# Expert stage of a gated transformer block: gate and up products made transposed, with fewer copies on VectorE and 39 tiles in place of 40

## The chip, the core and the metric

The kernel runs on one core of a Trainium2 chip. The metric is the device time of one execution in microseconds (us); three runs of the kernel before gave 368.71, 369.37 and 370.10 us, median 369.37. Below, PE is TensorE, DVE is VectorE, ACT is ScalarE, POOL is GpSimd and SP is SyncE. An engine has a sequencer, which works through the engine's instruction stream in order (waits, register arithmetic, branches, and handing matmuls on), and the datapath behind it.

## What is computed

```
x = x + tanh(g_xattn[0]) * xattn_0(layernorm(x), ctx, Wq, Wkv)
x = x + tanh(g_ffn[0])   * ffn_0(layernorm(x), Wr, Wqkv, Wo)      # per expert: top 64 tokens, attention
x = x + tanh(g_xattn[1]) * xattn_1(layernorm(x), ctx, ctx, mask, Wq, Wk, Wv, Wo)
x = x + tanh(g_ffn[1])   * ffn_1(layernorm(x), ...)
# ffn_1, the stage that the change touches:
normed = (xt - mu) * rsqrt(var + 1e-5) * ln_gamma + ln_beta        # 2048 tokens of 128
probs  = softmax(normed @ router_w.T)                              # 8 experts
top_v, top_i = top_k(probs, 2);  gates = softmax(top_v)
for e in range(8):                                                 # gate_up_w[e]: (768, 128), down_w[e]: (128, 384)
    gate, up = split(normed @ gate_up_w[e].T)
    out += comb[:, e] * ((silu(gate) * up) @ down_w[e].T)
out += swiglu(normed, shared_gate_up_w, shared_down_w)
```

## The kernel before

Everything lives in one program; each engine has its own instruction stream, and the streams meet only through semaphores. After the second cross attention each token's normalised row is split into two float16 halves (a high part and a rest), and POOL sends it by indirect DMA (`send_rows`, L787) into a table in DRAM, `dispatched_rows`, one region for each expert. From the counts of each expert DVE works out which expert each tile of 128 rows belongs to (L1040 to L1072), packs the numbers of eight tiles into one word (`te_i`), and PE reads that word into a register. So the expert of a tile is known only at run time.

The expert stage then works through 40 tiles of 128 rows (4096 routed rows, with each expert's share rounded up to whole tiles). The weights are held in SBUF as a high and a low float16 part (`wh`, `wl`), and every product of two float32 operands is made of three float16 matmuls: high by high, high by low, low by high. The address of a weight slice is `w[:, ds(expert, 1), ...]` with the expert in a register, so PE's sequencer works out each address with register instructions that stand in the stream just before the matmul that needs it. For each group of three matmuls there are two such addresses (`wa` and `wb`). For one tile the work is, in order:

- SP (`load_slots`, L470 to L476) loads the 128 rows (`slot_rows`, four buffers), after the tile four before has been transposed and its destination made.
- PE (`step_pe`, L1453) transposes the two halves (2 matmuls, L1462); DVE copies them out to `slot_rows_t` (L1115).
- PE makes gate and up, tokens on the partitions: for each of the two, three matmuls of 384 columns (L1473 to L1475; in the profile all of them have the helper's line, L1160, and `slot_rows_t` as an operand). The rows are the stationary operand, the weights the moving one. This makes 2 groups of three and 4 addresses.
- ACT (`step_act`, L669) applies silu to gate (L681); DVE (`step_dve`, L1093) multiplies by up (L1128); ACT rounds the product to its high half (L676); DVE makes the rest (L1118).
- PE transposes the two halves of the product in 6 matmuls (L1482), since the hidden dimension has to be on the partitions for the next product; ACT copies them out (`region_x`, 128x768, L686).
- PE makes the down product in 9 matmuls of 128 columns (L1492 to L1494, helper line L1160, operand `region_x`): 3 groups of three and 6 addresses.
- DVE scales and copies the result (L1108) and makes the destination row numbers (L1100, L1123, L1110); POOL writes the rows back to DRAM by indirect DMA (L814, `expert_rows`). Rows that only pad a tile go to a dump area behind the 4096 real ones.

The order in each stream is written out by hand as a software pipeline. PE's step s holds, in this order, the row transposes of tile s+4, gate and up of tile s+3, the product's transposes of tile s+1 and the down product of tile s. Steps -4 to 7 are unrolled, with constants in the waits; steps 8 to 35 are a hardware loop of four steps in a round (L1513), where the thresholds of the waits are in registers too, with a load of the next packed word once in a round; the last steps are unrolled again. Behind the stage PE makes the second half of the shared expert (`shared_pe(SH, B)`, L1520), SP loads the written rows back (`region_q`), and DVE and POOL add them, weighted, to x (L1151), which is stored.

Of the kernel before, what the change touches and what calls it, by code (L numbers as in the profile page):

```python
# [9 lines left out]
I32 = mybir.dt.int32  # L10
# [23 lines left out]
TILES = 40  # L34
TTAB = TILES + 8
# [58 lines left out]
def build(nc, x_in, ctx_in, mask_in, gx_in, gf_in, wq0_in, wkv0_in, wr0_in, wv0_in, wo0_in, wk1_in,  # L94
# [3 lines left out]
    ytok = nc.dram_tensor("expert_rows", (2 * B * S + TILES * P + 1, D), F32).ap()  # L98
# [4 lines left out]
    with ExitStack() as ctx:  # L103
# [141 lines left out]
        tw = sb("tile_window", [P, TILES // 4, 8])  # L245
        tpack = sb("tile_pack", [P, TILES // 4])
        te_i = sb("tile_pack_i", [P, TILES // 4], I32)
# [7 lines left out]
        dbase = sb("slot_dest_base", [P, 1])  # L255
        dall = sb("slot_dest_of", [P, TILES])
        dst = sb("slot_dest", [P, 4], I32)
# [4 lines left out]
        hidt = xf[:, 0:2 * FF].bitcast(F16).rearrange("p (r n) -> p r n", r=2)  # L262
        xt_ps = bank[4][:, 0:P].bitcast(F16)
        ht_ps = bank[5][:, 0:FF].bitcast(F16)
# [138 lines left out]
        dest_base = sem("dest_base")  # L403
        rows_turned = sem("rows_turned")
        rows_turned_out = sem("rows_turned_out")
        gate_up_made = sem("gate_up_made")
# [3 lines left out]
        hidden_turned = sem("hidden_turned")  # L410
        hidden_turned_out = sem("hidden_turned_out")
# [17 lines left out]
        def _(eng):  # L429
# [50 lines left out]
            with eng.Fori(1, TILES // 4) as i:  # L480
                for r in range(4):
                    load_slots(4 * i + r, r)
            for r in range(4):
                eng.wait_ge(rows_sent[r], 16 * (TILES // 4))
# [12 lines left out]
        def _(act):  # L497
# [171 lines left out]
            def step_act(s, u):  # L669

                static = isinstance(s, int)
                if not static or 0 <= s + 2 < TILES:

                    act.wait_ge(hidden_done, s + 3)
                    wait(act, hidden_turned, s + 1)
                    act.activation(hsplit[:, u % 2, 0:FF], hid[:, u % 2, :], ACT.Copy).then_inc(hidden_high, 1)  # L676
                if not static or 0 <= s + 3 < TILES:
                    act.wait_ge(gate_up_made, s + 4)
                    wait(act, hidden_done, s + 2)
                    v = (u + 3) % 2  # L680
                    act.activation(sil[:, v, :], bank[2 * v][:, 0:FF], ACT.Silu, scale=1.0 / WS).then_inc(silu_done, 1)  # L681
# [6 lines left out]
            for s in range(-4, 8):  # L688
                step_act(s, s % 4)
            with act.Fori(2, TILES // 4 - 1) as i:  # L690
                for u in range(4):
                    step_act(4 * i + u, u)
            for s in range(TILES - 4, TILES + 1):
# [15 lines left out]
        def _(pool):  # L709
# [97 lines left out]
            due = pool.alloc_register("tiles_due")  # L807
            pool.reg_mov(due, 1)
            with pool.Fori(0, TILES // 4):
                for r in range(4):  # L810

                    pool.wait_ge(rows_ready, due)
                    pool.reg_add(due, due, 1)
                    pool.indirect_dma_start(ytok, bass.IndirectOffsetOnAxis(dst[:, r:r + 1].bitcast(U32), 0),  # L814
                                            yv[:, r, :], None).then_inc(rows_sent[r], 16)
# [10 lines left out]
        def _(dve):  # L826
# [127 lines left out]
            for stage, t in skewed(NT, C_EVERY, C_DVE):  # L954
# [51 lines left out]
                elif stage == "route" and t % T == T - 1:  # L1006
# [9 lines left out]
                    dve.tensor_copy(pay[:, n, D + 1], ef[:, :, 0])  # L1016
# [44 lines left out]
            for h in range(2):  # L1061
                last = dve.tensor_scalar(tw[:, :, 4 * h:4 * h + 4],
                                         te[:, 4 * h:4 * h + TILES].rearrange("p (i j) -> p i j", j=4),
# [3 lines left out]
                                   c32[:, C_P8:C_P8 + 8].rearrange("p (a j) -> p a j", a=1).to_broadcast((P, TILES // 4, 8)),  # L1067
# [533 lines left out]
```

## Time and profile before

| what | us |
|---|---|
| median of three runs | 369.37 |
| span of the profiled execution | 368.7 |
| PE busy (matmuls) | 274.0 |
| DVE busy | 251.1 |
| ACT busy | 213.6 |
| POOL busy | 151.1 |
| first gate and up matmul of the expert stage | starts at 252.75 |
| last gate and up matmuls (tile 39) | start at 340.29 |
| last indirect DMA of the stage | starts at 348.02 |

```text
span 368.7 us, 7937 instructions
## 1 busy us (share of the span) xinstructions
PE 274.0 (74%) x2143; PEld 202.4 (55%) x2144; DVE 251.1 (68%) x884; ACT 213.6 (58%) x503; POOL 151.1 (41%) x201
## 2 busy tenths in 40 slices
PE   3499880395899876899897862536999999999810
PEld 2398780153677554577575751223776676776510
DVE  3256259996577631778889966833988788887475
ACT  1555549775577595845763534301877777777430
POOL 2412358960222510811732677760344444444502
PEclk9999996589899968999898855655999999999975
DMA  7860000620000000000000011221222122221173
GB/s 187 272 260 0 3 0 9 221 93 0 3 1 2 1 2 0 3 0 2 0 3 7 32 52 44 88 75 44 53 59 63 54 58 58 58 58 36 46 239 103
DMA packets 19469, 21.06 MB, mean 57 GB/s; under 512 B 3184, under 2 KB 17008, under 8 KB 18800
## 3 DMA queue, kind: packets, MB, share of 16 engines
q1 hardware_dynamic: 16992, 15.79, 14.1%
q0 software_dynamic: 2304, 4.77, 4.0%
q8 instruction: 14, 0.23, 0.3%
q10 hardware_dynamic: 144, 0.15, 0.2%
q14 instruction: 15, 0.12, 0.1%
HBM read 14.28 MB, written 6.42 MB: 56 GB/s over the span
## 4 chain that ended last, share of the span: by engine, by line
PE 54%; DVE 18%; issue 7%; POOL 7%; DMA 5%; ACT 5%; SPq 2%; DVEq 0%; POOLq 0%; ACTq 0%
PE bank L1160 43%; POOL dispatched_rows L787 5%; PE bank L1482 3%; DVE x L1151 2%; DMA region_q<-expert_rows 2%; DMA wr<-in 2%; DVE region_k L883 2%; PE bank L1462 2%; DVE region_k L967 2%; DVE top L882 2%; DVE nm L965 1%; ACT x_hat L514 1%; PE bank L1213 1%; PE bank L1196 1%; DVE bn_raw L838 1%
## 5 line engine op out<-in xcount | busy, mean ns | idle before, releaser
L814 POOL DMA_INDIRECT expert_rows<-region_k,slot_dest x40 | 38.2, 955 | 63.3 <-DVE slot_dest L1110 62.4
L1160 PE MATMUL bank<-w_high,slot_rows_t 128*128 x160 | 47.2, 337 | 3.2 <-issue 1.9
L681 ACT ACTIVATE region_w<-bank 128x384 f32<-128x384 f32 x40 | 19.6, 490 | 35.6 <-PE bank L1160 34.8
L787 POOL DMA_INDIRECT dispatched_rows<-region_t,slot x32 | 31.9, 997 | 16.1 <-issue 9.2
L1160 PE MATMUL bank<-w_high,region_x 128*128 (+1 forms) x272 | 35.8, 228 | 2.3 <-DVE region_t L908 2.1
L1128 DVE SCALAR_TENSOR_TENSOR region_w<-bank,region_w 128x384 f32<-128x384 f32 x40 | 22.3, 557 | 16.4 <-ACT region_w L681 15.3
L686 ACT ACTIVATE region_x<-bank 128x768 f16<-128x768 f16 x40 | 32.2, 804 | 0.9 <-PE bank L1482 0.9
L729 POOL TENSOR_SCALAR minus_mean_rstd<-mean_var 128x4 f32<-128x4 f32 x16 | 3.4, 213 | 71.1 <-DVE mean_var L841 45.7
L740 POOL TENSOR_TENSOR w_low<-w_scaled,w_high 128x512 f16<-128x512 f32 (+1 forms) x23 | 29.0, 1286 | 0.0
L514 ACT ACTIVATE x_hat<-x,minus_mean_rstd,rstd 128x128 f32<-128x128 f32 x64 | 26.2, 482 | 4.4 <-POOL minus_mean_rstd L732 4.4
L1160 PE MATMUL bank<-w_low,region_x 128*128 (+1 forms) x136 | 27.1, 227 | 0.0
L1160 PE MATMUL bank<-w_low,slot_rows_t 128*128 x80 | 26.9, 336 | 0.0
L1160 PEld LDWEIGHTS bank<-w_high,region_x 128*128 128x128 f16 x272 | 23.7, 98 | 3.2 <-issue 2.6
L1160 PEld LDWEIGHTS bank<-w_high,slot_rows_t 128*128 128x128 f16 x160 | 16.0, 100 | 14.4 <-issue 8.6
L1118 DVE TENSOR_TENSOR region_k<-region_w,region_k 128x384 f16<-128x384 f32 x40 | 22.3, 557 | 1.5 <-ACT region_k L676 1.4
L772 POOL TENSOR_TENSOR region_w<-region_k,rope_b 128x128 f32<-128x128 f32 x16 | 7.4, 463 | 36.4 <-DVE rope_b L926 36.4
L676 ACT ACTIVATE region_k<-region_w 128x384 f16<-128x384 f32 x40 | 20.9, 523 | 1.6 <-DVE region_w L1128 1.2
L1482 PE MATMUL bank<-c,region_k 128*128 128x128 f16 x240 | 19.9, 219 | 0.7 <-ACT region_x L686 0.7
L1482 PEld LDWEIGHTS bank<-c,region_k 128*128 128x128 f16 x240 | 16.6, 98 | 5.9 <-issue 1.0
L1160 PEld LDWEIGHTS bank<-v_blocks,region_k 128*128 128x128 f32 x128 | 17.9, 216 | 3.1 <-ACT region_k L631 1.7
L1160 PE MATMUL bank<-v_blocks,region_k 128*128 128x36 f32 x128 | 18.5, 295 | 0.8 <-DVE region_x L976 0.7
L634 ACT ACTIVATE region_k<-region_k 128x512 f32<-128x512 f32 x16 | 10.0, 628 | 15.6 <-DVE region_k L967 15.6
(238 smaller groups left out, 785.0 us busy)
## 6 DMA issues: line engine op xcount, KB each, us to landing
w_scaled<-in SPq DMA_DIRECT2D x5, 1024.0 KB, 8.2
slot_rows<-dispatched_rows SPq DMA_DIRECT2D x40, 65.5 KB, 1.9
region_q<-expert_rows SPq DMA_DIRECT2D x4, 512.0 KB, 5.7
x<-in SPq DMA_DIRECT2D x4, 256.0 KB, 4.4
region_w<-in SPq DMA_DIRECT2D x2, 512.0 KB, 6.9
out<-x SPq DMA_DIRECT2D x4, 256.0 KB, 2.6
w_scaled<-in SPq DMA_DIRECT2D x1, 704.0 KB, 4.0
expert_rows<-region_k,slot_dest POOLq DMA_INDIRECT x40, 2.2
```

The source lines that it names most:

```text
L514: last = act.activation(xh[:, t, :], x[:, t, :], ACT.Identity, bias=nmr[:, t:t + 1], scale=rstd[:, t:t + 1])
L634: act.activation(e1[:, t % 2, :], e1[:, t % 2, :], ACT.Exp, scale=HD ** -0.5).then_inc(cross1_exp, 1)
L676: act.activation(hsplit[:, u % 2, 0:FF], hid[:, u % 2, :], ACT.Copy).then_inc(hidden_high, 1)
L681: act.activation(sil[:, v, :], bank[2 * v][:, 0:FF], ACT.Silu, scale=1.0 / WS).then_inc(silu_done, 1)
L686: act.activation(hidt[:, (u + 1) % 2, :], ht_ps, ACT.Copy).then_inc(hidden_turned_out, 1)
L740: pool.tensor_tensor(wl[:, c], wf[:, r], wh[:, c], ALU.subtract).then_inc(w_low_done, 1)
L787: pool.indirect_dma_start(disp, bass.IndirectOffsetOnAxis(slot[:, b * T + t, c:c + 1].bitcast(U32), 0), pay[:, b * T + t, :], None).then_i ...
L814: pool.indirect_dma_start(ytok, bass.IndirectOffsetOnAxis(dst[:, r:r + 1].bitcast(U32), 0), yv[:, r, :], None).then_inc(rows_sent[r], 16)
L1118: dve.tensor_tensor(hsplit[:, u % 2, FF:2 * FF], hid[:, u % 2, :], hsplit[:, u % 2, 0:FF], ALU.subtract).then_inc(hidden_low, 1)
L1128: dve.scalar_tensor_tensor(hid[:, v, :], bank[2 * v + 1][:, 0:FF], 1.0 / WS, sil[:, v, :], ALU.mult, ALU.mult).then_inc(hidden_done, 1)
L1160: return pe.matmul(o, l, r, start=start, stop=stop)
L1482: last = pe.transpose(ht_ps[:, i * P:(i + 1) * P], hsplit[:, (u + 1) % 2, i * P:(i + 1) * P], ident16)
```

## The change

Of the expert stage and its tables only:

- Gate and up are made transposed: the weights are now the stationary operand and the rows the moving one. The 768 columns of gate and up are cut into 6 pieces of 128, and each piece is a group of three matmuls of 128 columns, with a `wa` and a `wb` of its own. The result has the hidden dimension on the partitions.
- The six transposes of the product, the copy behind them (L686) and its two semaphores are gone; the down product reads `hsplit` itself.
- The copy of the transposed rows moves from DVE to ACT, and the bank that holds them is doubled (banks 4 and 5), for which PE waits once, ahead of the stage, for the shared expert's first sums (`sh_added`).
- The pipeline is one step shorter: row transposes of tile s+3, gate and up of s+2, down of s. Silu waits for gate alone (`gate_made`), the product for up (`up_made`).
- The destination is one instruction on POOL (`slot_dest`) for each tile, two tiles ahead, and the three instructions on DVE are gone. POOL's loop is unrolled. Padding rows get a row number above the last real one, and the indirect DMA skips them (`bounds_check`).
- 39 tiles in place of 40 (the largest number that 4096 rows in 8 experts can need); the last round has three steps.

```
-TILES = 40
-TTAB = TILES + 8
+TILES = (2 * B * S + E * (P - 1)) // P
+ROUNDS = -(-TILES // 4)
+TTAB = 4 * ROUNDS + 8
...
             def step_act(s, u):
+                if not static or 0 <= s + 3 < TILES:
+                    act.wait_ge(rows_turned, s + 4)
+                    wait(act, up_made, s + 2)
+                    act.activation(xdt[:, (u + 1) % 2, :], xt_ps[(u + 1) % 2], ACT.Copy).then_inc(rows_turned_out, 1)
+                if not static or 0 <= s + 1 < TILES:
+                    act.wait_ge(hidden_done, s + 2)
+                    wait(act, down_made, s)
+                    act.activation(hsplit[:, (u + 1) % 2, 0:FF], hid[:, (u + 1) % 2, :], ACT.Copy).then_inc(hidden_high, 1)
                 if not static or 0 <= s + 2 < TILES:
...
-                    act.wait_ge(hidden_turned, s + 2)
-                    wait(act, down_made, s)
-                    act.activation(hidt[:, (u + 1) % 2, :], ht_ps, ACT.Copy).then_inc(hidden_turned_out, 1)
...
+            def slot_dest(n):
+                pool.wait_ge(rows_loaded[n % 4], n // 4 * 16 + 16)
+                pool.tensor_scalar(dst[:, n:n + 1], xd[:, n % 4, D + 1:D + 2], te[:, n:n + 1], xd[:, n % 4, D:D + 1],
+                                   ALU.is_equal, ALU.add).then_inc(dest_ready, 1)
+            slot_dest(0)
+            slot_dest(1)
+            for n in range(TILES):
+                if n + 2 < TILES:
+                    slot_dest(n + 2)
+                pool.wait_ge(rows_ready, n + 1)
+                pool.wait_ge(dest_ready, n + 1)
+                pool.indirect_dma_start(ytok, bass.IndirectOffsetOnAxis(dst[:, n:n + 1].bitcast(U32), 0),
+                                        yv[:, n % 4, :], None, bounds_check=2 * B * S - 1, oob_is_err=False).then_inc(rows_sent[n % 4], 16)
...
-            def step_pe(s, u, expert, expert3):
+            def step_pe(s, u, expert, expert2):
...
-                    for i in range(2):
-                        o = bank[2 * v + i][:, 0:FF]
-                        wa, wb = (w[:, ds(expert3, 1), i * FF:(i + 1) * FF].rearrange("p e n -> p (e n)") for w in gu_w)
-                        mm(o, xa, wa, True, False)
-                        mm(o, xa, wb, False, False)
-                        last = mm(o, xb, wa, False, True)
-                    last.then_inc(gate_up_made, 1)
-                if not static or 0 <= s + 1 < TILES:
-                    pe.wait_ge(hidden_low, s + 2)
-                    wait(pe, hidden_turned_out, s + 1)
-                    for i in range(2 * FC):
-                        last = pe.transpose(ht_ps[:, i * P:(i + 1) * P], hsplit[:, (u + 1) % 2, i * P:(i + 1) * P], ident16)
-                    last.then_inc(hidden_turned, 1)
+                    for i in range(NF):
+                        o = bank[2 * v + i // FC][:, i % FC * P:(i % FC + 1) * P]
+                        wa, wb = (w[:, ds(expert2, 1), i * P:(i + 1) * P].rearrange("p e n -> p (e n)") for w in gu_w)
+                        mm(o, wa, xa, True, False)
+                        mm(o, wa, xb, False, False)
+                        last = mm(o, wb, xa, False, True)
+                        if i == FC - 1:
+                            last.then_inc(gate_made, 1)
+                    last.then_inc(up_made, 1)
                 if not static or 0 <= s < TILES:
-                    pe.wait_ge(hidden_turned_out, s + 1)
+                    pe.wait_ge(hidden_low, s + 1)
                     wait(pe, rows_ready, s - 1)
...
-                        hi = hidt[:, u % 2, i * P:(i + 1) * P]
-                        lo = hidt[:, u % 2, FF + i * P:FF + (i + 1) * P]
+                        hi = hsplit[:, u % 2, i * P:(i + 1) * P]
+                        lo = hsplit[:, u % 2, FF + i * P:FF + (i + 1) * P]
...
+            pe.wait_ge(sh_added, SH)
```

## Rows read from the trace of the kernel before

**Rows 1.** Waits, 263 to 335 us, PE and ACT: total us, times, longest.

```profile
PE bank L1160 <- issue: 1.5, 9, 0.2
...
ACT region_w L681 <- PE bank L1160: 18.5, 31, 1.1
```

**Rows 2.** Chain that ended last, in order of time: start, length, what.

```profile
261.04 1.15 PE bank L1160 x6
...
269.20 1.04 PE bank L1160 x6
...
303.90 1.15 PE bank L1160 x6
...
313.05 1.15 PE bank L1160 x6
```

**Rows 3.** Timeline of PE in one loop step: start, length, line, operation, tiles, idle before.

```profile
315.05 0.33 PE L1160 MATMUL bank<-w_high,slot_rows_t 128*128 x1
315.22 0.33 PE L1160 MATMUL bank<-w_low,slot_rows_t 128*128 x1
...
317.26 0.23 PE L1462 MATMUL bank<-c,slot_rows 128*128 128x128 f16 x1 [0.23 <-issue]
```

**Rows 4.** Source line L1160, 303.9 to 322.2 us: register instructions of two rounds.

```profile
L1160 PEldq ALU_OP  x66: 32/36/36, 303.9 to 322.0; - x66
...
L1160 PEldq FUSED_REGOPS  x40: 46/46/60, 304.0 to 322.1; - x40
```

**Rows 5.** Source line L424, the wait helper, same stretch.

```profile
L424 PEldq EVENT_SEMAPHORE  x18: 51/51/51, 306.4 to 321.6; - x18
L424 PEldq ALU_OP  x14: 32/32/36, 304.3 to 321.8; - x14
```

**Rows 6.** Timeline: a down product (register addresses), then the shared expert (fixed addresses).

```profile
344.85 0.22 PE L1160 MATMUL bank<-w_low,region_x 128*128 x1
...
345.33 0.22 PE L1160 MATMUL bank<-w_low,region_x 128*128 x1
...
350.99 0.22 PE L1160 MATMUL bank<-w_low,region_k 128*128 128x128 f16 x1
...
351.16 0.22 PE L1160 MATMUL bank<-w_low,region_k 128*128 128x128 f16 x1
```

**Rows 7.** Groups of ACT and DVE, 303.9 to 322.2 us: busy, mean ns | idle before.

```profile
L676 ACT ACTIVATE region_k<-region_w 128x384 f16<-128x384 f32 x9 | 4.7, 523 | 0.0
L681 ACT ACTIVATE region_w<-bank 128x384 f32<-128x384 f32 x8 | 3.9, 491 | 5.0 <-PE bank L1160 5.0
...
L1128 DVE SCALAR_TENSOR_TENSOR region_w<-bank,region_w 128x384 f32<-128x384 f32 x8 | 4.5, 558 | 3.4 <-ACT region_w L681 3.2
L1118 DVE TENSOR_TENSOR region_k<-region_w,region_k 128x384 f16<-128x384 f32 x8 | 4.4, 556 | 0.0
L1108 DVE TENSOR_SCALAR region_k<-bank 128x128 f32<-128x128 f32 x8 | 2.3, 287 | 0.0
```

**Rows 8.** Timeline of POOL: small instructions between two indirect DMAs.

```profile
219.77 0.19 POOL L729 TENSOR_SCALAR minus_mean_rstd<-mean_var 128x4 f32<-128x4 f32 x1 [0.23 <-DVE mean_var L987]
...
221.78 1.10 POOL L787 DMA_INDIRECT dispatched_rows<-region_t,slot  x1 [0.16 <-issue]
```

**Rows 9.** Timeline: end of the stage.

```profile
340.29 0.34 PE L1160 MATMUL bank<-w_high,slot_rows_t 128*128 x1
...
348.02 0.96 POOL L814 DMA_INDIRECT expert_rows<-region_k,slot_dest  x1 [0.30 <-issue]
```

**Rows 10.** Timeline: start of the stage, gate and up of tile 0.

```profile
252.75 0.50 PE L1160 MATMUL bank<-w_high,slot_rows_t 128*128 x1
...
253.37 0.85 PE L1160 MATMUL bank<-w_high,slot_rows_t 128*128 x2
```

**Rows 11.** Stretches: busy and count of PE, PEld, DVE, ACT, POOL; granted clock.

```profile
89.25:92.66 3.41, 1.34 (x21) 1.16 (x20) 2.49 (x4) 0.00 (x0) 0.00 (x0) 1.00 0.00 0
92.66:96.08 3.42, 3.10 (x20) 2.44 (x19) 1.11 (x6) 1.30 (x7) 0.90 (x2) 0.50 0.00 0
```

More of the change, by code:

```diff
@@ L261, in build @@
         hsplit = region_k[:, 0:2, 0:FF].bitcast(F16)
-        hidt = xf[:, 0:2 * FF].bitcast(F16).rearrange("p (r n) -> p r n", r=2)
-        xt_ps = bank[4][:, 0:P].bitcast(F16)
-        ht_ps = bank[5][:, 0:FF].bitcast(F16)
+        xt_ps = [bank[4 + r][:, 0:P].bitcast(F16) for r in range(2)]
         yv = region_k[:, 2, :].rearrange("p (r n) -> p r n", r=4)
@@ L482, in _ @@
                     load_slots(4 * i + r, r)
+            for n in range(TILES // 4 * 4, TILES):
+                load_slots(n, n % 4)
             for r in range(4):
-                eng.wait_ge(rows_sent[r], 16 * (TILES // 4))
+                eng.wait_ge(rows_sent[r], 16 * len(range(r, TILES, 4)))
             for b in (0, B - 1, *range(1, B - 1)):
@@ L671, in step_act @@
                 static = isinstance(s, int)
-                if not static or 0 <= s + 2 < TILES:
[L674 to L681, printed above, removed]
-                if not static or 0 <= s + 1 < TILES:
-                    act.wait_ge(hidden_turned, s + 2)
-                    wait(act, down_made, s)
-                    act.activation(hidt[:, (u + 1) % 2, :], ht_ps, ACT.Copy).then_inc(hidden_turned_out, 1)
-            for s in range(-4, 8):
+                if not static or 0 <= s + 3 < TILES:
[6 more added lines that the diff above has]
+                    act.activation(hsplit[:, (u + 1) % 2, 0:FF], hid[:, (u + 1) % 2, :], ACT.Copy).then_inc(hidden_high, 1)
+                if not static or 0 <= s + 2 < TILES:
+                    act.wait_ge(gate_made, s + 3)
+                    wait(act, hidden_done, s + 1)
+                    act.activation(sil[:, u % 2, :], bank[2 * (u % 2)][:, 0:FF], ACT.Silu, scale=1.0 / WS).then_inc(silu_done, 1)
+            for s in range(-3, 8):
                 step_act(s, s % 4)
-            with act.Fori(2, TILES // 4 - 1) as i:
+            with act.Fori(2, ROUNDS - 1) as i:
                 for u in range(4):
                     step_act(4 * i + u, u)
-            for s in range(TILES - 4, TILES + 1):
+            for s in range(4 * (ROUNDS - 1), TILES):
                 step_act(s, s % 4)
@@ L1460, in step_pe @@
                     for h in range(2):
[L1461 to L1462 removed]
+                        w = xd[:, r, h * (D // 2):(h + 1) * (D // 2)].bitcast(F16)
+                        last = pe.transpose(xt_ps[r % 2][:, h * P:(h + 1) * P], w, ident16)
                     last.then_inc(rows_turned, 1)
[L1464 to L1468 removed]
+                if not static or 0 <= s + 2 < TILES:
+                    pe.wait_ge(rows_turned_out, s + 3)
+                    wait(pe, hidden_done, s + 1)
+                    v = u % 2
@@ L1500, in _ @@
             load_window(1)
-            for s in range(-4, 4):
-                step_pe(s, s % 4, e[max(s, 0)], e[max(s + 3, 0)])
+            pe.wait_ge(sh_added, SH)
+            for s in range(-3, 4):
+                step_pe(s, s % 4, e[max(s, 0)], e[max(s + 2, 0)])
             def round_pe(i, ahead):
                 e = experts()
-                for u in range(4 if ahead else 5):
-                    step_pe(4 * i + u, u % 4, e[u], e[u + 3])
+                for u in range(4 if ahead else TILES - 4 * i):
+                    step_pe(4 * i + u, u, e[u], e[u + 2])
                     if ahead and u == 1:
```

92 lines of the change are left out of this document (30 added, 62 removed).

## Prediction

> **What bounds the kernel now.** The page first: in the slices of the expert stage (252 to 348 us) PE stands at 9 of 10, DVE at 7 to 8, and PE's clock is fully granted. So PE is the engine to look at, and the question is what in PE. The waits of the stage come next [rows 1]: ACT waits for PE (18.5 us), while PE waits for another engine hardly at all; what idle time it has is called "issue". The chain of the end then gives the pace. From one loop round to the next, tile by tile at the same place, 303.90 to 313.05, are 9.15 us for four tiles, 2.29 each; in the unrolled rounds 261.04 to 269.20 are 8.16 us, 2.04 each [rows 2]. The array doesn't need that much. Matmuls of 384 columns start 0.17 us apart [rows 3] and those of 128 columns with fixed addresses 0.17 us for three, 0.056 each [rows 6]. A tile has 6 of the first kind and 17 of the second (2 row transposes, 6 transposes of the product, 9 of down): 6 x 0.17 + 17 x 0.056 = 1.97 us. Some 0.32 us in each loop tile is neither array nor wait for an engine; a part of it is seen as a gap ahead of the next tile's first matmul, 0.23 us at 317.26, released by nothing [rows 3].
>
> What fills it is PE's sequencer. Line L1160 holds, in two rounds, 66 + 40 register instructions, and the wait helper another 32 instructions [rows 4, 5]. The price of those is seen where PE has nothing queued. At the end of the stage the down product of one tile, three groups of three matmuls with two addresses each, has its w_low matmuls at 344.85 and 345.33, two groups apart, so 0.24 us for a group; the same three matmuls with fixed addresses, in the shared expert, take 0.17 (350.99 to 351.16) [rows 6]. A group with register addresses can't be issued faster than 0.24 us. Now the sum for a round: 20 groups (5 a tile) x 0.24 = 4.8 us, 32 transposes at no more than 0.056 = 1.8 us, and 106 + 32 - 80 = 58 further register and wait instructions in two rounds, 29 in one, besides the load of the next word and the branch, for the 2.55 us that remain: under 0.09 us each, against 0.24 - 0.17 = 0.07 visible for the two in a group. The round is full. I read the stage as bound by PE's sequencer, with the array fed from a queue that the long 384-column matmuls fill and the short ones empty.
>
> **The change, part by part, per tile.**
> - Gate and up: 2 groups become 6, so 4 groups more, + 4 x 0.24 = +0.96 us of sequencer. For the array 6 x 0.17 = 1.02 become 18 x 0.056 = 1.01: nothing.
> - The six product transposes go: at most 6 x 0.056 = 0.34; at least nothing, as a matmul without an address may cost the sequencer little. I take 0.17.
> - Of eight waits in PE's step two go (for the copy behind those transposes and ahead of down). Each is worth 0 (it rides on an instruction that stays) to 0.09; I take 0.1 for both.
> - Net +0.69 a tile, with ends of +0.96 (nothing given back) and +0.96 - 0.34 - 0.18 = +0.44. Loop tiles go from 2.29 to 2.98 (2.73 to 3.25), unrolled ones from 2.04 to 2.73.
> - The load of the packed word and the branch stay once in a round.
> - ACT loses the 0.8 us copy and gets the copy of 256 columns, no more than its 0.49 for 384 [rows 7]: at most 0.49 + 0.52 + 0.49 = 1.5 us a tile. DVE keeps 0.56 + 0.56 + 0.29 = 1.41 [rows 7]. Both lie under the pace; they cost nothing as long as it is above 1.5.
> - POOL: 0.96 for the DMA, then 0.23 to a small instruction, 0.19 for it, and 0.16 to the next DMA [rows 8, 9], 1.54 a tile with the destination. What is queued behind a wait there is only the next tile's send. The bounds check isn't in the trace; a tile may cost 0 to 0.5 more and is hidden up to 2.9, by PE. SP's loads wait for that destination of four tiles before, some three steps (9 us) ahead of use: hidden; at a pace of 1.6 it would be near.
> - Skipped padding rows (some 900 of 4992) take writes away that nobody waits for: nothing. The wait for `sh_added` stands ahead of rows that land at 251.5, and POOL's first two destinations stand behind its last dispatch: nothing.
> - A shorter pipeline: down of a tile comes two steps (6 us) after its gate; silu, product and split take 0.49 + 0.56 + 0.52 + 0.56 = 2.1 [rows 7]. Hidden.
>
> The stage. Tile 0's gate and up start at 252.75 as now [rows 10]. The first two steps hold gate and up alone and run at the half clock: 384 columns take 0.31 there (252.75 to 253.37 for two [rows 10]), so 128 take 0.105, and 18 + 2 of them 2.1; two steps 4.2. Then 36 steps reach tile 38's gate and up: 8 unrolled x 2.73 = 21.8, 28 in the loop and behind it x 2.98 = 83.4. That is 362.2 us, where the last one starts at 340.29 now [rows 9]: +21.9 us. From there to the last indirect DMA are 7.73 us now [rows 9]. After: 6 groups 1.44, then 0.2 for the result, 0.56 + 0.52 + 0.56 (silu is done by then) with three handovers of 0.05, down 0.72 + 0.2, copy 0.29, and 0.5 until POOL's DMA starts: 5.2 us. That gives 2.5 back; POOL's queue at the end (0.30 idle, a DMA behind a DMA, [rows 9]) is gone too. The last DMA starts at 367.4 in place of 348.02, +19.4 us; what follows (landing, load, sum, store) is the same. Profiled execution: 368.7 + 19.4 = 388.1; the median of the runs is 0.7 above the span, so 389 us.
>
> The Trainium skill has two rules here, and they don't agree. "TensorE: Matmul & The Clock Gate", section "Wait — 56ns, not 53.3ns?", has a warm matmul cost its columns at 2.4 GHz and 2.5 ns; by it 29 matmuls of 128 columns are an estimated 1.62 us a tile, and the stage is far faster than now (the first rival). The section "Back-to-back issue gap" of that page of the Trainium skill gives about 81 ns for each 128-column matmul with its weight load; by it a tile takes an estimated 29 x 0.081 = 2.35 us, much as now (the third rival). The fixed-address rows agree with the first (0.056) and not with the second; neither section knows of address arithmetic.
>
> **The rivals.**
> - *The array sets the pace* (the side of faster). If the address arithmetic of gate and up overlaps with matmuls that are queued, a tile costs 29 x 0.056 = 1.62 us, above POOL's 1.54. Tile 38 starts at 252.75 + 4.2 + 36 x 1.62 = 315.3, the last DMA at 320.5: 27.5 us earlier, 342 us. For it: in steady state today's down products do run at the array's pace, since 384-column matmuls fill the queue ahead of them. Against it: after the change there are no long matmuls left to fill it, and the loop round is already longer than the array needs. It decides from the pace at which both kernels are equal: (348.02 - 5.2 - 252.75 - 4.2) / 36 = 2.39 us a tile. Below that the change is a gain.
> - *The clock falls.* The array has work for 1.62 of 2.98 us. At 89.25 to 92.66 us PE was busy for 1.34 of 3.41 us at the full clock, and the next stretch ran at half, 1.2 in place of 2.4 GHz [rows 11]. At half clock a tile is 29 x 0.105 = 3.05 us of array, and with what the queue can't hide 3.1 to 3.3: 36 x 0.25 = 9 us at the most behind the forecast, 394 to 398 us. Against it: PE had been idle for over half of the stretch before that drop, in long waits, and has only short gaps here; and the half clock, if it comes, leaves the array no gaps.
> - *Only the groups count.* If waits and the other register instructions lie beside matmuls, a tile is 9 x 0.24 + 2 x 0.056 = 2.27 us, 2.44 with the word's load and the branch (about 0.7 a round). At 2.27 the last DMA starts at 343.9 (365 us), at 2.44 at 350.0 (371 us); 368 us in the middle, no change. Against it: the same reckoning gives 1.65 a tile now, where 2.29 are measured.
> - *The change doesn't do what it says*, in that two addresses for each piece are made with fewer register instructions than in down: it would fall in with the third or the first case.
>
> **How the numbers follow.** Forecast (sequencer, 2.98 a tile): 0.66. Clock falls: 0.12. Groups only: 0.06. Array: 0.16, the fourth case among it. The forecast's own range follows from 2.73 to 3.25 in the loop: -9 and +10 us, 380 to 399 with the clock's case inside it. I take 379 to 399, which leaves out the two fast cases and little else. What a measurement can tell from no change is 0.5%, 1.8 us. Slower by more: 0.66 + 0.12 + 0.02 = 0.80; within: 0.04; faster: 0.16.
>
> **What the profile would show.** Right: PE's busy share in the stage falls, the w_low matmuls of the gate and up groups (`slot_rows_t`) stand about 0.24 us apart, loop rounds of some 12 us, PE's idle time still called "issue", DVE, ACT and POOL idle a good half. L1160 has 9 fused register instructions a tile. Wrong: three matmuls of gate and up in 0.17 us throughout and a round under 9.5 us; or ACT or POOL with no idle time; or a granted clock of 0.5 in the stage, which makes the second rival out of the forecast. The prediction hangs on one number, the 0.24 us for a group with two register addresses, read at the end of the stage, and on its holding for addresses of the stationary operand too, which the trace of before doesn't show.

## The result, and the profile after

Slower: a median of 397.99 us (396.41 to 399.08, four runs) where the kernel before, beside it on the same chip, took 369.74 (368.71 to 371.25, four runs). The ratio is 1.073, 95% interval 1.067 to 1.080. The profiled execution of after is 394.6 us long, that of before 368.7. The forecast was a profiled execution of 388.1 and a median of 389 us.

The first look is the page of after, its slices (tenths busy in 40 slices of 9.9 us; the stage is slices 26 to 38).

```profile
span 394.6 us, 8358 instructions
...
PE   3599760786998468998798362498888888888830
...
DVE  4156179975677317887998674154444445444566
ACT  2555559682776868466554421253333434333330
POOL 3313179911225108034347877135545454545412
PEclk9999995698999979998895556599999999999975
```

PE stays the busiest engine, at 8 of 10 now; DVE fell from 7 or 8 to 4 or 5 and ACT to 3 or 4. TensorE's clock was fully granted from slice 27 to the end of the stage (1.00, the level of 2.4 GHz, from 263 to 362 us), so the half clock of the rival has no part in the loss.

The chain that ended last gives the pace. Columns: start, length, what. One place of the loop's round comes back as the first three rows:

```profile
299.66 1.58 PE bank L1147 x18
...
312.32 1.57 PE bank L1147 x18
...
324.97 1.57 PE bank L1147 x18
...
368.74 1.54 PE bank L1147 x18
...
375.02 2.11 DMA expert_rows<-region_k,slot_dest
```

A round of four tiles is 12.65 us, 3.16 a tile, where [rows 2] have 9.15 and 2.29. Tile 0's gate and up start at 252.65, where [rows 10] have 252.75; the last gate and up start at 368.74 and the last indirect DMA at 375.02, where [rows 9] have 340.29 and 348.02: 28.4 and 27.0 us later.

What PE waits for is in the waits of the stage, 270 to 360 us (total, times, longest):

```profile
ACT slot_rows_t L673 <- PE bank L1450: 46.9, 29, 2.1
POOL expert_rows L816 <- DVE region_k L1112: 42.7, 28, 2.1
DVE region_k L1115 <- ACT region_k L678: 25.3, 28, 1.3
...
PE bank L1147 <- issue: 8.3, 37, 0.3
```

ACT, POOL and, through ACT, DVE wait for PE; PE has gaps only for "issue": in 90 us now 8.3 at these matmuls and 4.6 at the row transposes (L1450), where in 72 us before has 1.5 [rows 1] and 1.6 (L1462). The rest of the loss is no gap in this view: it lies between the groups. The timeline of PE, one tile's gate and up:

```profile
359.54 0.22 PE L1147 MATMUL bank<-slot_rows_t,w_low 128*128 128x128 f16 x1
...
359.78 0.22 PE L1147 MATMUL bank<-slot_rows_t,w_low 128*128 128x128 f16 x1
...
360.01 0.22 PE L1147 MATMUL bank<-slot_rows_t,w_low 128*128 128x128 f16 x1
...
360.74 0.22 PE L1147 MATMUL bank<-slot_rows_t,w_low 128*128 128x128 f16 x1
```

Each of the six groups of three matmuls has one w_low matmul; they stand 0.24 us apart, as in the down product of before, and not 0.17 as with fixed addresses [rows 6]. A busy row of 0.22 us hides this: the matmuls overlap in the array, and only the distance between starts tells. The source line of the matmuls, two rounds (299.66 to 324.95 us), shows what stands between them:

```profile
L1147 PEldq ALU_OP  x94: 32/32/36, 299.7 to 324.7; - x94
L1147 PEldq FUSED_REGOPS  x72: 46/46/60, 299.8 to 324.9; - x72
```

Nine fused instructions a tile, one for each group, where [rows 4] have five. The same view of a part of one tile's gate and up (359.55 to 360.75 us) shows when they start:

```profile
L1147 PEldq FUSED_REGOPS  x5: 46/46/46, 359.6 to 360.5; - x5
L1147 PEldq ALU_OP  x5: 32/32/32, 359.7 to 360.6; - x5
```

Five of each kind in turn, from 359.6 to 360.6 us: a fused one every 0.24 us and an ALU_OP halfway between. So a register instruction starts about every 0.12 us all through the groups, though its own row is only 32 or 46 ns long. What fills the rest of the 0.12 us isn't shown.

### The profile page after: what moved, and what is told of

It reads as the page before. It is cut to its first block, busy times and chain, and to the rows that moved or that the text cites. A ratio compares the mean times of both kernels' runs of the same rounds, so it can differ in the third digit from the quotient of the medians.

```text
span 394.6 us, 8358 instructions
## 1 busy us (share of the span) xinstructions
PE 287.0 (73%) x2354; PEld 211.1 (53%) x2355; DVE 233.2 (59%) x721; ACT 197.5 (50%) x500; POOL 173.5 (44%) x239
## 4 chain that ended last, share of the span: by engine, by line
PE 56%; DVE 16%; issue 10%; ACT 6%; POOL 6%; DMA 5%; SPq 2%; DVEq 0%; POOLq 0%; ACTq 0%
PE bank L1147 48%; POOL dispatched_rows L783 5%; PE bank L1450 2%; DMA wr<-in 2%; DVE x L1138 2%; DMA region_q<-expert_rows 2%; DVE region_k L885 2%; DVE region_k L969 1%; DVE top L884 1%; DVE nm L967 1%; ACT x_hat L511 1%; ACT w_high L523 1%; PE bank L1200 1%; PE bank L1183 1%; ACT w_scaled L521 1%
## 5 line engine op out<-in xcount | busy, mean ns | idle before, releaser
L1147 PE MATMUL bank<-slot_rows_t,w_high 128*128 128x128 f16 x468 | 59.2, 227 | 8.5 <-issue 8.5
L1147 PE MATMUL bank<-slot_rows_t,w_low 128*128 128x128 f16 x234 | 52.0, 223 | 0.0
L673 ACT ACTIVATE slot_rows_t<-bank 128x256 f16<-128x256 f16 x39 | 14.9, 383 | 67.2 <-PE bank L1450 67.2
L1147 PE MATMUL bank<-w_high,region_k 128*128 (+1 forms) x266 | 39.2, 230 | 11.3 <-DVE region_k L1085 7.3
L1115 DVE TENSOR_TENSOR region_k<-region_w,region_k 128x384 f16<-128x384 f32 x39 | 24.0, 615 | 32.2 <-ACT region_k L678 32.2
L1147 PEld LDWEIGHTS bank<-slot_rows_t,w_high 128*128 x468 | 28.3, 100 | 24.9 <-issue 14.7
L1147 PEld LDWEIGHTS bank<-w_high,region_k 128*128 128x128 f16 x266 | 26.0, 100 | 20.5 <-issue 9.7
L1147 PE MATMUL bank<-w_low,region_k 128*128 (+1 forms) x133 | 29.8, 225 | 0.0
L1147 PEld LDWEIGHTS bank<-slot_rows_t,w_low 128*128 x234 | 23.0, 98 | 0.4
L1450 PE MATMUL bank<-c,slot_rows 128*128 128x128 f16 x78 | 11.1, 224 | 12.9 <-DMA slot_rows<-dispatched_rows 7.9
L1112 DVE TENSOR_SCALAR region_k<-bank 128x128 f32<-128x128 f32 x39 | 11.3, 291 | 13.1 <-PE bank L1147 13.0
```

The costliest lines, as they stand in the source:

```text
L673: act.activation(xdt[:, (u + 1) % 2, :], xt_ps[(u + 1) % 2], ACT.Copy).then_inc(rows_turned_out, 1)
L1112: dve.tensor_scalar(yv[:, r, :], bank[6 + r % 2][:, 0:D], 1.0 / WS, None, ALU.mult).then_inc(rows_ready, 1)
L1115: dve.tensor_tensor(hsplit[:, v, FF:2 * FF], hid[:, v, :], hsplit[:, v, 0:FF], ALU.subtract).then_inc(hidden_low, 1)
L1147: return pe.matmul(o, l, r, start=start, stop=stop)
L1450: last = pe.transpose(xt_ps[r % 2][:, h * P:(h + 1) * P], w, ident16)
```

## The experiments

The theory that stands to be tested: PE's sequencer sets the pace of the stage in both kernels, and the two register instructions of each group are what it spends its time on. The rivals: the array sets it; the group count has nothing to do with it, and another part of the change lost the time; the waits and the loop are what costs. "Pace" below is the distance between the same rows of two rounds in the chain, divided by four.

**1 to 3: the addresses taken away.** In three kernels the weights are read at a fixed address, always those of the first expert, so nearly all of PE's register instructions in the groups fall away and nothing else changes. In the first, of after, for all groups:

```
-wa, wb = (w[:, ds(expert2, 1), i * P:(i + 1) * P]...   gate and up
+wa, wb = (w[:, 0:1, i * P:(i + 1) * P]...
-wa, wb = (w[:, ds(expert, 1), i * D:(i + 1) * D]...    down
+wa, wb = (w[:, 0:1, i * D:(i + 1) * D]...
```

> The changed kernel, but every weight slice of the expert stage is read at the fixed address of expert 0, so no address of a matmul stands in a register; the same matmuls, waits, copies and DMAs. What it leaves out: the right expert's weights (the routed sum is made with expert 0's). Theory (PE's sequencer with its register instructions sets the pace): a group of three matmuls goes from 0.24 to 0.17 us, the loop tile from 3.16 us to the next bound, which by this kernel's trace is POOL with 1.18 + 0.38 + 0.23 + 0.16 = 1.95 us: some 36 x 1.15 = 41 us less, about 357 us. Rival A (it is the number of 128-column matmuls and weight loads, at 0.08 us each): at least 29 x 0.08 = 2.3 us a tile, 367 us or more. Rival B (ACT, DVE or a load sets the pace): no change, 398 us.

In the second, of after, for gate and up alone:

> The changed kernel with fixed addresses (expert 0) for the gate and up weights alone; the down product keeps its register addresses. What it leaves out: the right expert's gate and up weights. Theory: 12 of the 18 register instructions for addresses go, 6 groups x (0.24 - 0.06) = 1.05 us of sequencer a tile: 3.16 to 2.1 us, 36 x 1.05 = 38 us less, about 360 us. Rival A (matmul count): as in the kernel with all addresses fixed. Rival B: no change.

In the third, of before, for all groups (its `expert3` and FF columns in place of `expert2` and P):

> The kernel before with the fixed addresses of expert 0 for all weights. What it leaves out: the right expert's weights. Theory: the sequencer loses 10 address instructions a tile, and the array becomes the bound at 6 x 0.163 + 17 x 0.056 = 1.93 us, with DVE's 1.9 close to it: 2.24 to about 2.0 us, 39 x 0.24 = 9 us less, about 360 us. Rival (the stage before was bound by the array or by DVE's chain and not by the sequencer): no change, within 1 us of 369.5.

Measured, in two executions each, beside 371.89 us for the kernel before: 355.93 us (ratio 0.957, 0.944 to 0.970), 358.02 (0.962, 0.946 to 0.979) and 358.48 (0.964, 0.950 to 0.978). In all three the rivals, with 367 or 398 us for the first two and no change for the third, are outside. So the whole loss of the change, and more, hangs on the addresses: by the ratios (1.073 and 0.957 of 371 us) after is some 43 us faster without them than with them, before 13. With gate and up alone freed, 41 of the 43 are back. The chain of before with fixed weights shows an even pace that the array sets:

```profile
294.16 0.98 PE bank L1160 x6
296.08 0.97 PE bank L1160 x6
298.01 0.97 PE bank L1160 x6
```

1.92 us a tile; the prediction had worked out 1.97 for what the array needs. From 263 to 325 us PE is busy throughout and waits for nothing; DVE, busy for 59.8 of the 62 us, is close behind. After with fixed weights ran at the array's pace in a few tiles only:

```profile
265.60 1.51 PE bank L1147 x27
267.33 1.51 PE bank L1147 x27
268.97 1.51 PE bank L1147 x27
```

267.33 to 268.97 is 1.64 us for the 29 matmuls of a tile, 0.057 each; the first rival had 1.62. The w_low matmuls of gate and up, whose weights are the stationary operand, stand 0.17 us apart here, where the changed kernel has 0.24:

```profile
265.55 0.22 PE L1147 MATMUL bank<-slot_rows_t,w_low 128*128 128x128 f16 x1
265.72 0.22 PE L1147 MATMUL bank<-slot_rows_t,w_low 128*128 128x128 f16 x1
```

The section "Back-to-back issue gap" of the page "TensorE: Matmul & The Clock Gate" of the Trainium skill, about 81 ns for such a matmul with its weight load, would make that an estimated 2.35 us; this row doesn't agree, and the 0.24 us for three in the changed kernel, which looks like it, is gone as soon as the addresses are. But this pace didn't last. POOL in the same kernel, 263 to 330 us (count | busy, mean ns | idle before):

```profile
L816 POOL DMA_INDIRECT expert_rows<-region_k,slot_dest x35 | 39.6, 1133 | 11.4 <-POOL slot_dest L806 7.4 <-DVE region_k L1112 3.2 <-issue 0.8
L806 POOL TENSOR_SCALAR slot_dest<-slot_rows,tile_expert 128x1 int32<-128x1 f32 x34 | 15.4, 452 | 1.7
```

35 tiles in 67 us, 1.91 each, and of the 67 POOL waits 3.2 for the result of another engine. Its DMA, its destination and the handover between the two fill the rest, and the row loads, which wait for the destinations, now come late for PE (waits, 270 to 330 us):

```profile
PE bank L1450 <- DMA slot_rows<-dispatched_rows: 5.1, 8, 1.3
```

So the part of the change that moved the destinations to POOL costs nothing in the changed kernel, where PE hides it, and would be the next bound at 1.9 us a tile if PE were faster.

**4: register additions in before**, four in each step, ahead of gate and up:

```
+for _ in range(4):
+    pe.reg_add(idle, idle, 1)
```

> The kernel before with four more register additions on PE in each tile's step (a register that nothing reads), ahead of gate and up; the same matmuls and the same output. Theory: each costs the sequencer about 0.1 us and all of it is on the path: 40 x 0.4 = +16 us, about 385 us. Rival (the sequencer has slack): 0 to +2 us, 370 us.

Measured: 371.88 us beside 371.89, ratio 1.000 (0.996 to 1.005). It isn't a test. The source line of the groups has 66 ALU_OP and 40 FUSED_REGOPS rows in two rounds (296.33 to 314.76 us), as without the edit [rows 4]: the compiled program doesn't hold the additions, whose result nobody reads. It says only that two builds of the same work agree.

**5: waits in before**, for a count reached long ago:

```
+for _ in range(4):
+    pe.wait_ge(tiles, 3)
```

> The kernel before, with four waits added on TensorE at the start of every step of the expert loop; what they wait for is long reached, so nothing is held up but the sequencer. If TensorE's sequencer sets the pace and a wait costs it about 0.1 us, the loop's tiles go from 2.29 to about 2.6 us and the time rises by 10 to 16 us, to some 383 us where the kernel before takes 370. If the instructions between the groups lie beside the array's work (the array needs 1.9 us a tile), nothing changes: 370 us.

Measured: 377.99 us beside 372.06, ratio 1.017 (1.012 to 1.021); pace 9.94 us a round (299.84 to 309.78) in place of 9.15. The direction is the theory's, and an instruction that holds nothing up but the sequencer costs time; but it is 0.79 us for the 16 waits added to a round, 0.05 each and not 0.1. The compiled loop doesn't hold 16 more instructions. In two rounds (299.84 to 309.78 is one):

```profile
L1469 PEldq EVENT_SEMAPHORE  x20: 51/51/51, 301.5 to 319.3; - x20
L424 PEldq EVENT_SEMAPHORE  x14: 51/51/51, 302.4 to 318.9; - x14
```

These are 34 where [rows 5] have 18, with the 14 ALU_OP of that line unchanged: 8 more in a round, 0.10 us for each. The chain of this run goes through ACT's silu and DVE's product in some tiles, where it puts PE's gap down to L1128. That isn't a wait: the matmuls of 307.15 stand behind the product of two tiles before, which began at 303.74 and took 0.56 us.

**6 and 7: the loop written out.** PE's rounds 2 to 8, in before and in after; the upper bound is `TILES // 4 - 1` in before and `ROUNDS - 1` in after:

```
-with pe.Fori(2, ...) as i:
+for i in range(2, ...):
```

> The kernel before, with TensorE's loop over rounds 2 to 8 written out step by step: the same groups, waits and expert numbers in registers, but no jump and no threshold that has to be computed into a register. Theory of the sequencer: the 28 tiles go from 2.29 us each to the 2.04 us of the steps that were written out already, 7 us less, 362 to 363 us. Rival (the array, or a chain through the other engines, sets the pace): no change.

> The changed kernel with the same edit. Its loop tiles take 3.16 us, its written-out ones 2.85 to 3.05. Theory of the sequencer: 28 tiles x 0.2 = about 6 us less, 391 to 392 us, and still far above the kernel before, because the addresses in the groups stay. If the loop were the whole of the loss, it would come back to 370 us.

Measured: before 367.44 us beside 372.06 (0.988, 0.984 to 0.993), after 393.81 (1.057, 1.049 to 1.066). Before gains 4.6 us (1.2%) where 7 were expected; its pace is 8.92 a round (292.52 to 328.21 are four rounds), so 2.23 a tile and not 2.04. Written out, a round has 71 instructions of the sequencer's in place of 74, counted over all lines, so there was little to gain. After went from 1.073 to 1.057 of before, in two different comparisons, some 6 us, with 12.1 us a round in place of 12.65. So the loop itself is a small part of the pace in both kernels, and no part of the difference between them.

**8: fewer steps in before**: rounds written out, two covered waits of each step dropped, the expert's number kept in a register for the down product three steps later.

```
+if 0 <= s + 3 < TILES:
+    held[s + 3] = expert3 = pe.snap(expert3, min_val=0, max_val=E - 1)
+if 0 <= s < TILES:
+    expert = held.pop(s)
...
-pe.wait_ge(rows_turned_out, s + 4)
+if s + 4 >= TILES:
+    pe.wait_ge(rows_turned_out, s + 4)
...
-pe.wait_ge(hidden_turned_out, s + 1)
+if s + 1 >= TILES:
+    pe.wait_ge(hidden_turned_out, s + 1)
```

> The kernel before with the rounds written out, two waits of each step left out that another wait of the same step already covers, and each tile's expert number put into a register once and kept for the down projection three steps later. Theory of the sequencer: below the 2.04 us a tile of the written-out steps, by about 0.1 us, with a floor at the 1.92 us of the kernel with fixed weights: 358 to 361 us, and faster than both kernels. Rival: the kept registers or code that grows long cost as much as they save, and it stays at the 362 us of the written-out kernel or above.

Measured: 361.71 us, ratio 0.975 (0.970 to 0.980), faster than both kernels, with nothing left out. The chain:

```profile
303.30 1.15 PE bank L1160 x6
...
311.47 1.15 PE bank L1160 x6
```

8.17 us for four tiles, 2.04 each, with 56 + 40 + 16 instructions of the sequencer's in two rounds where the written-out kernel of run 6 has 66 + 40 + 32. That is 13 fewer in a round for 0.75 us; it is 0.12 us a tile above the array's 1.92, so part of what was saved was no longer on the path.

**9: the small groups alone.** This run takes from the change only the number of groups. The rows stay stationary, the transposes, copies and waits stay; the 384 columns are made in three groups of 128.

```
-for i in range(2):
-    o = bank[2 * v + i][:, 0:FF]
-    wa, wb = (w[:, ds(expert3, 1), i * FF:(i + 1) * FF]...
+for i in range(NF):
+    o = bank[2 * v + i // FC][:, i % FC * P:(i % FC + 1) * P]
+    wa, wb = (w[:, ds(expert3, 1), i * P:(i + 1) * P]...
```

> The kernel before, with nothing changed but the cut of gate and up: the rows stay the stationary operand, but the 384 columns of each product are made in three groups of 128, so six groups a tile in place of two, with twelve register addresses in place of four. Columns for the array, transposes, copies and waits are as before. Theory of the sequencer: 4 more groups x 0.24 = 0.96 us a tile, loop tiles of 3.25 us, and 38 of them 36 us more: about 408 us, slower than the changed kernel. Rival (the array sets the pace, or the loss lies in the other parts of the change): 370 to 375 us.

Measured: 405.44 us beside 370.6, ratio 1.091 (1.084 to 1.099). The chain and, under it, the source line of two rounds:

```profile
300.04 1.65 PE bank L1160 x18
...
364.77 1.68 PE bank L1160 x18
```

```profile
L1160 PEldq ALU_OP  x98: 32/32/36, 300.1 to 325.8; - x98
...
L1160 PEldq FUSED_REGOPS  x72: 46/46/60, 300.2 to 325.9; - x72
```

300.04 to 364.77 are five rounds of 12.95 us: 3.24 a tile, 0.95 more than before. The columns that the array has to stream are the same. Four groups cost 0.95 us, 0.24 each, and they bring exactly 16 ALU_OP and 16 fused instructions in a round more than [rows 4], so 0.119 us for one register instruction. They also bring 12 more matmuls and weight loads a tile, which this run can't tell from the addresses; runs 1 and 2, where as many matmuls without addresses run at 0.057 us each, and run 10 can. With them it is settled: one part of the change makes the whole loss and more, and it makes it in a kernel that has nothing else of the change.

**10: one address instead of two.** In after, gate and up read the low half of the weights at a fixed address, that of the first expert; what this leaves out is the right expert's low half.

```
-wa, wb = (w[:, ds(expert2, 1), i * P:(i + 1) * P]... for w in gu_w)
+wa = gu_w[0][:, ds(expert2, 1), i * P:(i + 1) * P]...
+wb = gu_w[1][:, 0:1, i * P:(i + 1) * P]...
```

> The changed kernel, in which gate and up read the low half of the weights at a fixed address (so always those of the first expert) and the high half at the expert's: one register address a group in place of two, the same matmuls. With both fixed the kernel took 358 us, with both in registers 398. If each register instruction costs its own time, about 0.09 us, the six fewer of a tile give 0.5 us back: loop tiles of about 2.6 us, 378 to 381 us. If a group pays once for having any register address (a queue that is emptied), it stays at about 398 us.

Measured: 372.48 us beside 370.6, ratio 1.005 (1.001 to 1.009). The chain has one round at

```profile
301.45 1.74 PE bank L1147 x27
...
311.34 1.74 PE bank L1147 x27
```

9.89 us, 2.47 a tile in place of 3.16. The six register instructions that a tile has less are worth 0.69 us, 0.115 each; I had expected 0.5 (0.09 each). That the cost goes by instruction and not by group is shown, with the number of matmuls unchanged, and its size agrees with that of run 9. In its source line the fused ones are 72 as in after and the ALU_OP 46 in place of 94: the second address of a group is the ALU_OP, the first the fused one.

**11: 39 tiles**, on top of run 8, the part of the change that could help: the tables, the loads, the sends and the last rounds for 39 tiles, groups and destinations as in before.

```
-TILES = 40
+TILES = (2 * B * S + E * (P - 1)) // P
```

> The kernel before with fewer register steps (361.7 us beside 372 for the kernel before), and from the change only that 39 tiles are worked on in place of 40; TensorE's groups, the transposes and the destinations stay as they were. One step of 2.05 us falls away at the end of the stage: about 359.5 us, ratio 0.969 to the kernel before. Rival: the last tile's rows weren't what the end waited for, and it stays at 361.7 us, 0.975.

Measured: 358.08 us, ratio 0.966 (0.960 to 0.971), the fastest kernel that reads every expert's own weights. One step of 2.05 us is 0.6% of it; against run 8 (0.970 to 0.980, in another comparison) it is some 1% less, with intervals that just touch, so the gain of this step is likely and not proven.

**12: the six transposes given back to after**, without copy and wait:

```
+for i in range(2 * FC):
+    pe.transpose(bank[6 + u % 2][:, P:P + FF].bitcast(F16)[:, i * P:(i + 1) * P],
+                 hsplit[:, u % 2, i * P:(i + 1) * P], ident16)
```

> The changed kernel, to which the six transposes of the product are given back, into a part of the bank that nobody reads; they bring no wait, no copy and no register address. It prices by itself what the forecast took as 0.17 us a tile between ends of 0 and 0.34. If they cost the array's full time, 39 tiles take 13 us more, about 411 us; at the forecast's half of it 6.6 us, about 404; if the matmuls lie wholly beside the sequencer's work, nothing: 398 us. The kernel before with small groups (3.24 us a tile with transposes and waits, 3.16 after) speaks for under 0.1 us, so for 398 to 401 us.

Measured: 399.52 us beside 371.48, ratio 1.076 (1.072 to 1.080), where after had 1.073 (1.067 to 1.080). In the chain

```profile
299.81 1.56 PE bank L1147 x18
...
338.70 1.55 PE bank L1147 x18
```

three rounds take 38.89 us, 3.24 a tile in place of 3.16. Six transposes, 0.34 us of the array, are worth 0.08 us a tile here: most of them run while the sequencer works on addresses.

## Why the prediction was right, and where it was off

**The bound.** Right. A pace that the sequencer sets was read from a remainder of 0.32 us a tile that neither array nor engines explained, and from one number at the end of the stage. Runs 3, 5 and 8 move the pace of before by the sequencer's work alone (1.92, 2.49 and 2.04 in place of 2.29), runs 1, 9 and 10 that of after and of its groups.

**Four groups x 0.24.** Right: forecast 0.96 us a tile, measured alone 0.95 (run 9). That the price would hold for addresses of the stationary operand, which the trace of before couldn't show, is seen in the 0.24 between the w_low rows of after.

**What is given back.** This is the term that was mis-sized. The forecast took off 0.17 for the six transposes and 0.1 for two waits, 0.27 in all, and had 2.98 in the loop. After is at 3.16; the small groups in before are at 3.24. So everything else of the change gives back 0.08 us a tile, and run 12 finds just that for the transposes. The low end that I had named for the waits, nothing, is what happened. The wait helper (now L419) has 18 EVENT_SEMAPHORE rows in two rounds in after as in [rows 5] and 6 ALU_OP in place of 14, but the other 8 stand, for PE's other waits, on lines of their own, so it is 32 in both:

```profile
L1454 PEldq ALU_OP  x6: 32/32/32, 302.0 to 324.4; - x6
L1446 PEldq FUSED_REGOPS  x2: 46/46/46, 308.2 to 320.8; - x2
```

The step that was off is "at most the array's 0.34, at least nothing, I take half": in a stage that I had just called bound by the sequencer, the array's price of a matmul was the wrong end to lean on. The error is 28 x 0.18 = 5.0 us in the loop and 1.5 in the rest of the stage, together the 6.5 us by which the last gate and up came late (368.74 against 362.2).

Counted over all lines of PE's sequencer, the branch and the load of the next word among them, after has 208 instructions in two rounds and before 148: 30 more in a round, for 3.5 us more, 0.117 each, which accounts for the whole loss in the loop.

A small thing doesn't fit and stays open. Run 9 has 212, so after has 2 fewer in a round. At 0.119 these are 0.24 us, and run 12, which has the same transposes as run 9 and the same 208 instructions as after, should have a round shorter by that; its rounds are 12.96 us and those of run 9 are 12.95. Nor is the price the same for every kind: the waits of run 5 cost 0.10, and what run 8 took away gave 0.06 each.

**The tail.** From the last gate and up to the last indirect DMA the forecast had 5.2 us, it was 6.3. Two steps were off: "POOL's queue at the end is gone", and a product that goes straight on to ACT. The timeline of after's end:

```profile
370.37 0.56 DVE L1104 SCALAR_TENSOR_TENSOR region_w<-bank,region_w 128x384 f32<-128x384 f32 x1 [0.94 <-PE bank L1147]
...
371.38 0.52 ACT L678 ACTIVATE region_k<-region_w 128x384 f16<-128x384 f32 x1 [1.30 <-PE bank L1147]
...
372.39 1.06 POOL L816 DMA_INDIRECT expert_rows<-region_k,slot_dest  x1 [1.57 <-DVE region_k L1112]
372.42 0.28 DVE L1112 TENSOR_SCALAR region_k<-bank 128x128 f32<-128x128 f32 x1
...
373.56 0.29 DVE L1112 TENSOR_SCALAR region_k<-bank 128x128 f32<-128x128 f32 x1 [0.86 <-PE bank L1147]
...
373.75 0.97 POOL L816 DMA_INDIRECT expert_rows<-region_k,slot_dest  x1 [0.30 <-issue]
...
375.02 0.97 POOL L816 DMA_INDIRECT expert_rows<-region_k,slot_dest  x1 [0.30 <-issue]
```

The last result is there at 373.85 and its DMA starts 1.17 us later, behind two others, where the forecast had 0.5. That is 0.7 us; the other 0.4 come earlier. The last product is ready at 370.93, but ACT rounds it at 371.38 only, since the half of `hsplit` that it writes is still read by the down product of two tiles before. When nothing is left to slow PE, the last three down products follow each other faster than POOL can send them, in this kernel as in the one before. Against it the end came 1.1 us sooner than it should: 19.6 us from the start of the last DMA to the end, where before has 20.7, as that DMA lands in 2.11 us and not in 3.12. The sum: 6.5 + 1.1 - 1.1 = 6.5 us over the forecast, 394.6 against 388.1. That the last two cancel is luck.

**The median and the range.** The median was forecast at 389 and came out at 397.99, 9 us more. The 2.5 us beyond the 6.5 are the step from the profiled execution to the median, put at 0.7 us from the runs of before: the profiled execution of after was the shortest of the four (396.41 us, 394.6 in its profile), so the step was 3.4. The range of 379 to 399 held by 1 us, and one of the four runs (399.08) lies outside it; the way and the mechanism were forecast well, the size with little to spare.

**The hidden parts.** Right in that they cost nothing, wrong in one size. POOL was put at 1.54 us a tile and needs 1.9 (1.13 for the DMA and 0.45 for the destination on the average, the rest handovers), as run 1 shows. It would have broken the forecast's first rival: with the array at 1.62 us a tile POOL would have held the stage at 1.9, and the kernel would have come to the 356 us of run 1 and not to 342.

**The rivals.** *Array sets the pace*: refuted by the 0.24 of the groups, and its condition is shown in run 1, where taking the addresses away is what it needs. *Clock falls*: it didn't; the granted clock was 1.00 while PE's array had work for about half of each tile's 3.16 us. Its sum was wrong too: 3.1 to 3.3 us a tile are 0.12 to 0.32 above 2.98, so up to 11.5 us and 400, not 9 and 398. *Only the groups count* (2.27 to 2.44 a tile): refuted by 3.16. *The change doesn't do what it says*: it does, nine fused instructions a tile. The section "Wait — 56ns, not 53.3ns?" of "TensorE: Matmul & The Clock Gate" in the Trainium skill has about 56 ns for a warm matmul of 128 columns. The trace agrees where addresses are fixed, with the 1.64 us for 29 of run 1; the 3.16 us of after are set by something else.

## What to carry to other kernels

A matmul whose weight address is worked out in a register brings work to TensorE's sequencer, here 0.12 us for each register instruction. Small matmuls (0.056 us) don't hide it; long ones (0.17 us for 384 columns) hide a good part, as the 10 address instructions a tile of before cost 0.37 us in all (2.29 against 1.92 in run 3). So count addresses and groups, not columns, before cutting a wide product into narrow ones or turning its operands round; compare the distance of matmul starts in a group with register addresses to that in a group with fixed ones, in the same trace. And when a stage is bound by one resource, what is removed from another may give back next to nothing: six transposes were worth 0.08 us of their 0.34.

## What the hardware showed that I had not expected

- The indirect DMA of POOL takes longer when a small instruction of POOL stands before it. In after, 270 to 360 us, line, count | busy, mean ns:

```profile
L816 POOL DMA_INDIRECT expert_rows<-region_k,slot_dest x28 | 33.9, 1211 | 42.7 <-DVE region_k L1112 42.7
L806 POOL TENSOR_SCALAR slot_dest<-slot_rows,tile_expert 128x1 int32<-128x1 f32 x28 | 10.5, 375 | 1.5
```

1.21 us, where before has 0.955 on the average in its stage; the last two of after, with no destination between them, are back at 0.97 (the timeline above). These two have the bounds check as well, so the check alone doesn't explain it; how many rows they send, and so whether that plays a part, isn't known. The destination itself takes 0.375 us, twice the small instruction of [rows 8].
- DVE's split of the product (L1115) takes 0.63 us on the average in after and 0.56 at 368.87 and 371.94, where POOL makes no destination beside it; before had 0.56 [rows 7]. That it shares something with POOL's destination was not tried.
- The last indirect DMA lands in 2.11 us in the changed kernel and in runs 1, 7, 10 and 12, in 2.10 in run 2, and in 2.5 to 3.1 in all kernels made from before that show it in the chain. The skipped padding rows are the likely reason; no run separates it.
